# The skip term written by ScalarE, and the graph hops by Horner's rule

## The reference

```python
x = x + gnn(layernorm(x), adj, ...)
x = x + ffn(layernorm(x), ...)

def gnn(X, A, Wv, bv, aw, ab, Wk, bk):          # 3 hops
    Xw = X @ Wv + bv
    sj, si = Xw @ aw[:d, 0], Xw @ aw[d:, 0]
    e = leaky_relu(sj[:, None, :] + si[:, :, None] + ab[0], 0.2)
    alpha = A * exp(e)
    transition = alpha / (alpha.sum(-1, keepdims=True) + 1e-12)
    H, Xk = 0, X
    for k in range(3):
        H = H + Xk @ Wk[k] + bk[k]
        Xk = transition @ Xk
    return relu(H)

def ffn(...):                                   # fc1, Mamba, fc2
    u, z = split(W_in (W_fc1 x + b_fc1));  u = silu(causal_conv4(u) + conv_b)
    dt, B, C = split(W_xproj u);  delta = softplus(W_dt dt + b_dt)
    h_t = exp(delta_t A) h_{t-1} + delta_t u_t B_t        # 1024 channels x 16 states
    y_t = C_t h_t + D u_t;  y = y * silu(z)
    return W_fc2 W_out y + b_fc2
```

## Time and profile before

| | us |
|---|---|
| three runs | 4127.19, 4118.02, 4119.69 |
| median | 4119.69 |
| the profiled execution: its time | 4124.45 |
| its span, from the first to the last instruction | 4122.3 |
| mean granted PE clock | 0.95 of full speed |

### The profile page before, as it was taken

The page is one execution under the profiler, slowest core; times in us unless marked ns, Lnnn a source line. Parts: engine busy times, 40 slices in busy tenths (PEclk is TensorE's granted clock), DMA queues, the critical chain, the costliest instruction groups (busy, mean ns, idle before and its releaser), DMA issues. The chain is left out here.

```text
span 4122.3 us, 44370 instructions
## 1 busy us (share of the span) xinstructions
PE 3597.6 (87%) x11386; PEld 2046.1 (50%) x11386; DVE 3607.9 (88%) x3165; ACT 2868.8 (70%) x6098; POOL 3455.2 (84%) x1860
## 2 busy tenths in 40 slices
PE   6888888988888988888988888988888988888887
PEld 3644554545554545554544554554554554554443
DVE  0499988999989999889998989999999899989898
ACT  1577667777667777667777667777767777767775
POOL 0298888898888998888998888898888898888899
PEclk8899999999999999999999999999999999999999
DMA  2111101111101111101111101111101111101110
GB/s 100 49 51 53 53 9 47 50 53 53 53 8 48 50 53 53 53 8 48 50 53 53 53 8 48 50 53 53 53 9 47 50 53 53 53 8 44 47 47 8
DMA packets 50702, 183.68 MB, mean 45 GB/s; under 512 B 7339, under 2 KB 33203, under 8 KB 42067
## 3 DMA queue, kind: packets, MB, share of 16 engines
q1 hardware_dynamic: 48880, 174.17, 11.0%
q10 hardware_dynamic: 1636, 7.83, 0.5%
HBM read 164.15 MB, written 17.83 MB: 44 GB/s over the span
## 5 line engine op out<-in xcount | busy, mean ns | idle before, releaser
L411 POOL TENSOR_TENSOR st<-st,bc 128x1024 f32<-128x1024 f32 x1024 | 2399.4, 2358 | 474.2 <-DVE st L870 473.0
L870 DVE TENSOR_TENSOR_SCAN st<-dec,st 128x1024 f32<-128x1024 f32 x1024 | 2311.9, 2277 | 78.0 <-ACT dec L464 63.6
L464 ACT ACTIVATE dec<-delta,decay 128x254 f32<-128x254 f32 x4096 | 1695.1, 465 | 713.4 <-DVE st L870 712.4
L685 PE MATMUL y_ps<-st,ident 128*128 128x512 f32 x4096 | 1975.9, 611 | 184.2 <-POOL st L411 182.8
L685 PEld LDWEIGHTS y_ps<-st,ident 128*128 128x128 f32 x4096 | 756.5, 194 | 999.8 <-issue 599.7
L858 DVE TENSOR_TENSOR st<-du,bc 128x1024 f32<-128x1024 f32 x736 | 885.5, 1203 | 34.3 <-ACT du L450 34.3
L402 POOL TENSOR_TENSOR st<-du_sb,bc 128x1024 f32<-128x1024 f32 x288 | 679.3, 2359 | 0.1
L896 DVE SCALAR_TENSOR_TENSOR u<-d_ps,chan,u 128x250 f32<-128x250 f32 (+2 forms) x768 | 309.4, 473 | 160.9 <-ACT u L504 159.2
L705 PE MATMUL g<-wo,zs 128*128 128x256 f32 x1024 | 300.2, 446 | 0.8 <-DVE zs L877 0.8
L705 PEld LDWEIGHTS g<-wo,zs 128*128 128x128 f32 x1024 | 230.8, 229 | 128.8 <-issue 92.1
L681 PE MATMUL y_ps<-u,diag 128*128 128x256 f32 x512 | 168.5, 459 | 127.7 <-DVE zs L877 127.6
(11 more groups left out here) (106 smaller groups left out, 2775.1 us busy)
## 6 DMA issues: line engine op xcount, KB each, us to landing
bc<-bc_dram SPq DMA_DIRECT2D x64, 2048.0 KB, 9.8
xg<-x_dram SPq DMA_DIRECT2D x32, 256.0 KB, 11.5
x_dram<-xg SPq DMA_DIRECT2D x32, 256.0 KB, 2.0
last_x<-x_dram SPq DMA_DIRECT2D x32, 256.0 KB, 2.6
out_dram<-last_x SPq DMA_DIRECT2D x32, 256.0 KB, 2.1
bc<-w_inT_dram ACTq DMA_DIRECT2D x1, 4096.0 KB
adjt<-adjT_dram SPq DMA_DIRECT2D x32, 128.0 KB, 11.2
bc<-w_out_dram ACTq DMA_DIRECT2D x1, 2048.0 KB
```

The costliest lines, as they stand in the source:

```text
L411: nc.gpsimd.tensor_tensor(st[:, sl, :, :, :], st[:, sl, :, :, :], bc[:, p, 1, SU * q:SU * q + SU, None, :].to_broadcast([P, SU, 2, T]), AL ...
L464: a = nc.scalar.activation(dec[:, v % 2, s, j, :].rearrange("p (b t) -> p b t", b=PAIR)[:, :, 1:], delta[:, p, 2 * i + j, :].rearrange("p ...
L685: mm = nc.tensor.matmul(y_all, ident[:, :], st[:, sl, s, :, :].rearrange("p j t -> p (j t)"), start=False, stop=(q == Q - 1 and s == SU - ...
L870: nc.vector.tensor_tensor_scan(h, dec[:, v % 2, :, :, :].rearrange("p s j t -> p (s j t)"), h, 0.0, ALU.mult, ALU.add).then_inc(S["scanned ...
```

## The change

The skip term: at step 2 of each sum, behind the decays of that step, ACT writes `D u` for two channel blocks straight into `y_ps` with two Copy activations (`skip_term`), and PE's first identity matmul of the sum waits for that instead of for the gate. One matmul at the start (`prime`) has written all of the bank once, so that the identity matmuls add. `diag` and its construction go.

The graph stage: with A the attention divided by its row sums, H = b + X W0 + A (X W1 + A (X W2)). PE makes `X W2` (phase 9), ACT copies it (11), the logits move to phase 12, their two Exp to 14, maximum and product on DVE behind the scan of phase 15. The row sums are taken with a 128x128 matrix of ones (17), so that each partition holds them; DVE adds the small constant, takes the reciprocal and multiplies the attention, three operations on 128x256 (19, before the scan). `X W1 + A (X W2)` follows (21, 22), its copy (24), then `b + X W0 + A (...)` (25, 26), and DVE makes `x1` in one operation (28, before the scan). The row sums, the scaled copies and the transposed hops of before go.

```diff
@@ -49,6 +49,8 @@
 FOLD_OUT = (1, 3, 5, 7)
+PRIME_STEP = 25
+SKIP_STEP = 2
 EDGE_STEP = 8
...
@@ -449,6 +447,18 @@
+            def skip_term(act, k, p, i):
+                if i == 0:
+                    wait(act, "silu_u", k + 1)
+                    if isinstance(k, int) and k == 0:
+                        act.wait_ge(S["y_primed"], 1)
+                wait(act, "y_gated", JP * k + i)
+                for j in range(2):
+                    a = nc.scalar.activation(y_ps[:, j, :], u[:, p, 2 * i + j, :], ACT.Copy,
+                                             scale=chan[:, TAPS + 2, 2 * i + j:2 * i + j + 1])
+                a.then_inc(S["skipped"], 1)
             def decays(act, k, p, v):
                 i, q = v // Q, v % Q
@@ -474,6 +484,8 @@
                         decays(act, k, p, v + 1)
+                    if scan and v % Q == SKIP_STEP:
+                        skip_term(act, k, p, v // Q)
                     if dense:
...
                     if scan and v == SILU_Z:
@@ -546,10 +558,7 @@
                     wait(act, "rstd_made", 2 * g + 1 + second)
-                    if second:
-                        wait(act, "h_mm", g + 1)
-                    else:
-                        wait(act, "transposed", 2 * g)
+                    wait(act, "transposed", 2 * g + second)
                     for b in range(PAIR):
...
                                                  scale=rstd[:, b:b + 1])
@@ -559,31 +568,19 @@
                 if v == 11:
+                    wait(act, "x2k_mm", g + 1)
+                    nc.scalar.activation(x2k[:, :, :].rearrange("p b d -> p (b d)"), g0[:, :], ACT.Copy)\
+                        .then_inc(S["x2k_made"], 1)
+                if v == 14:
                     wait(act, "e_mm", g + 1)
-                    e_ps = g0[:, 0:PAIR * L].rearrange("p (b i) -> p b i", b=PAIR)
-                    nc.scalar.activation(att[:, :, :], e_ps, ACT.Exp, bias=c0[:, 0:1])
-                    nc.scalar.activation(g0[:, PAIR * L:2 * PAIR * L], g0[:, 0:PAIR * L], ACT.Exp, bias=c0[:, 1:2], scale=0.2)\
+                    nc.scalar.activation(att[:, :, :].rearrange("p b i -> p (b i)"), g0[:, 0:T], ACT.Exp, bias=c0[:, 0:1])
+                    nc.scalar.activation(g0[:, T:2 * T], g0[:, 0:T], ACT.Exp, bias=c0[:, 1:2], scale=0.2)\
                         .then_inc(S["e_exp"], 1)
-                if v == 19:
-                    wait(act, "rinv_made", g + 1)
-                    wait(act, "u1_mm", g + 1)
-                    for b in range(PAIR):
-                        a = nc.scalar.activation(x1k[:, b, :], g0[:, b * DIM:(b + 1) * DIM], ACT.Copy,
-                                                 scale=rinv[:, b:b + 1])
-                    a.then_inc(S["x1k_made"], 1)
-                if v == 22:
-                    wait(act, "u1T_mm", g + 1)
-                    nc.scalar.activation(u1T[:, :, :].rearrange("p c t -> p (c t)"), g0[:, :], ACT.Copy)\
-                        .then_inc(S["u1T_made"], 1)
                 if v == 24:
-                    wait(act, "u2T_mm", g + 1)
-                    nc.scalar.activation(u2T.rearrange("p c t -> p (c t)"), g0[:, :], ACT.Copy)\
-                        .then_inc(S["u2T_made"], 1)
-                if v == 26:
-                    wait(act, "h0_mm", g + 1)
+                    wait(act, "x1k_mm", g + 1)
                     nc.scalar.activation(x1k[:, :, :].rearrange("p b d -> p (b d)"), g0[:, :], ACT.Copy)\
-                        .then_inc(S["h0_made"], 1)
+                        .then_inc(S["x1k_made"], 1)
                 if v == 37:
                     wait(act, "transposed", 2 * g + 2)
@@ -648,6 +645,11 @@
+            def prime(pe):
+                wait(pe, "wo_folded", JP)
+                nc.tensor.matmul(y_all, ident[:, :], wxz[:, 0, 0:512], start=True, stop=True).then_inc(S["y_primed"], 1)
             def body(pe, k, p, scan, dense, ends, begins):
...
                 for v in range(U):
@@ -659,6 +661,8 @@
                         fold_wo(pe, v)
+                        if v == PRIME_STEP:
+                            prime(pe)
                     if scan:
...
                             project_out(pe, k - 1, r, OUT_STEPS.get(v, ()), ends)
@@ -673,13 +677,7 @@
                 if q == 0:
-                    wait(pe, "y_gated", JP * k + i)
-                    if isinstance(k, int) and k == 0 and i == 0:
-                        pe.wait_ge(S["diag_made"], J)
-                        pe.wait_ge(S["wo_folded"], JP)
-                    for j in range(2):
-                        nc.tensor.matmul(y_ps[:, j, :], diag[:, 2 * i + j, :], u[:, p, 2 * i + j, :],
-                                         start=(j == 0), stop=False, skip_group_check=True)
+                    wait(pe, "skipped", JP * k + i + 1)
                 wait(pe, "c_times", U * k + v + 1)
...
                     mm = nc.tensor.matmul(y_all, ident[:, :], st[:, sl, s, :, :].rearrange("p j t -> p (j t)"),
@@ -774,6 +772,12 @@
                     for b in range(PAIR):
+                        mm = hop(b, 2, True, True)
+                    mm.then_inc(S["x2k_mm"], 1)
+                if v == 12:
+                    wait(pe, "x2k_made", g + 1)
+                    for b in range(PAIR):
                         for c in range(KC):
...
                             nc.tensor.matmul(g0[:, b * L:(b + 1) * L], wi_rep[:, c, :], cols,
@@ -781,55 +785,39 @@
                     mm.then_inc(S["e_mm"], 1)
-                if v == 15:
+                if v == 17:
                     wait(pe, "alpha_made", g + 1)
-                    for b in range(PAIR):
-                        mm = nc.tensor.matmul(g0[:, b:b + 1], att[:, b, :], one_col[:, 0:1], start=True, stop=True)
-                    mm.then_inc(S["rowsum_mm"], 1)
-                if v == 17:
-                    wait(pe, "rinv_made", g + 1)
-                    for b in range(PAIR):
-                        mm = nc.tensor.matmul(g0[:, b * DIM:(b + 1) * DIM], att[:, b, :], xn[:, b, :],
-                                              start=True, stop=True)
-                    mm.then_inc(S["u1_mm"], 1)
-                if v == 20:
+                    nc.tensor.matmul(g0[:, 0:T], ones[:, :], att[:, :, :].rearrange("p b i -> p (b i)"),
+                                     start=True, stop=True).then_inc(S["rowsum_mm"], 1)
+                if v in (21, 22):
+                    b = v - 21
+                    wait(pe, "att_made", g + 1)
+                    hop(b, 1, True, False)
+                    mm = nc.tensor.matmul(g0[:, b * DIM:(b + 1) * DIM], att[:, b, :], x2k[:, b, :],
+                                          start=False, stop=True, skip_group_check=True)
+                    if b == 1:
+                        mm.then_inc(S["x1k_mm"], 1)
+                if v in (25, 26):
+                    b = v - 25
                     wait(pe, "x1k_made", g + 1)
-                    for c in range(KC):
-                        for b in range(PAIR):
-                            mm = nc.tensor.matmul(g0[:, c * T + b * L:c * T + (b + 1) * L],
-                                                  xn[:, b, c * P:(c + 1) * P], att[:, b, :], start=True, stop=True)
-                    mm.then_inc(S["u1T_mm"], 1)
-                if v == 22:
-                    wait(pe, "u1T_made", g + 1)
-                    for c in range(KC):
-                        for b in range(PAIR):
-                            mm = nc.tensor.matmul(g0[:, c * T + b * L:c * T + (b + 1) * L],
-                                                  x1k[:, b, c * P:(c + 1) * P], att[:, b, :], start=True, stop=True)
-                    mm.then_inc(S["u2T_mm"], 1)
-                if v == 24:
-                    wait(pe, "u2T_made", g + 1)
-                    nc.tensor.matmul(g0[:, :], ones3, bk_row, start=True, stop=False, skip_group_check=True)
-                    for b in range(PAIR):
-                        for c in range(KC):
-                            mm = nc.tensor.matmul(g0[:, b * DIM:(b + 1) * DIM], xT[:, c, b * L:(b + 1) * L],
-                                                  wks[:, 0, c, :], start=False, stop=(c == KC - 1),
-                                                  skip_group_check=True)
-                    mm.then_inc(S["h0_mm"], 1)
-                if v in (27, 28):
-                    b = v - 27
-                    wait(pe, "h0_made", g + 1)
-                    for n in range(2):
-                        for c in range(KC):
-                            mm = nc.tensor.matmul(g0[:, b * DIM:(b + 1) * DIM],
-                                                  (u1T, u2T)[n][:, c, b * L:(b + 1) * L], wks[:, 1 + n, c, :],
-                                                  start=(n == 0 and c == 0), stop=(n == 1 and c == KC - 1))
+                    if b == 0:
+                        nc.tensor.matmul(g0[:, :], ones3, bk_row, start=True, stop=False, skip_group_check=True)
+                    hop(b, 0, False, False)
```

(54 more changed lines are left out.)

## The result

The changed kernel takes 4197.12 us (median of 4 runs, 4195.41 to 4198.13) against 4120.6 for the kernel before in the same comparison: ratio 1.0183, 95% interval 1.0165 to 1.02. It is slower by 76 us, where the prediction had 46 us, inside its range.

The account below looks back on a forecast made before the run. No engine's total bounds the kernel; waits on DVE's clock set the pace. Per pair 6.85 - 2.25 + 0.5 - 3.5 = +1.6 us, over 29 pairs +46 us: median 4166 us, range 4070 to 4235, forecast chance 0.53.

Parts of the forecast that it names:

- a, the exponentials behind Ln: Units 24 to 26: exponentials moved behind Ln keep DVE waiting; scan of 27 only 0.25 us late.
- b, PE's gap: Units 25 to 29: PE idles 5.9 us for ACT's copy, loses 2.7 to lower clock; DVE waits 3.7 for row sum.
- b, the reciprocal: DVE at unit 29: reciprocal on 128x256 takes 2.1 us, the three operations together 2.9 us.
- Rival 2: Reciprocal costs like other operations, three operations 1.24 us: no change, 4118 us; chance 0.12.
- c, the waits of units 30 to 1 are swallowed: DVE's lateness absorbs the waits 0.72 and 1.53 us: -2.25 us a pair, 4.6 late at the first taps.
- d: Unit 2: copies replace the diagonal matmuls at equal time, but PE's longer idle time prolongs its lower clock: +0.5 us.
- e, the gain: Units 3 to 16: `x1` made earlier, PE's 5.36 us stall at the output projection goes: -3.5 us a pair.
- the gates at units 10 and 18 I cost at nothing: Skip copies at these gates elsewhere cost nothing; at 18 they run where PE's diagonal ran, within 0.1 us.
- Rival 1: Row sum in time at unit 29, wait 1.0 us: -1.1 us a pair, 4088 us, up to 4050; chance 0.20.
- W + R - 5.0: Change of a pair in us: W is the wait at unit 29, R the three DVE operations; no loss below 5.0.
- Rival 3: ACT becomes late: copies push the next decays by 0.85 us at three other places, +2.5 a pair, 4239 us; chance 0.15.

Follow-up runs that it names:

- the early row sum: The changed kernel with exponentials, maximum and product, row sum and the three DVE operations moved to earlier phases (13, 14, 15, 17): 4147 us, ratio 1.0078.
- the gap filled: The changed kernel with six idle 128x512 matmuls in PE's 5.8 us gap before the sum of unit 24: 4139 us, ratio 1.0054.
- the fastest version: New graph stage reordered, skip term on PE: 4034 us, ratio 0.9801 to the kernel before; with one POOL addition moved as well, 4029 us, ratio 0.9799.

## Why the prediction was right, and where it was off

- **a, the exponentials behind Ln.** Right: a wait of 2.18 us in the shown pair (2.0 by the working), +1.89 to the gate of 26.
- **b, PE's gap.** Right in place, cause and size: 5.80 us for 5.9 (unit 23 ends at 2133.0 by its row, not at 2132.84, which makes 5.75), the copy pair 0.86 for 0.85, wait for the row sum 107.7/32 = 3.4 for 3.7. That it costs time is shown by two runs, 58 us each. Not seen was the second way (Z, z bias, decays), which the early row sum shows.
- **b, the reciprocal.** 1.77 us for 2.1. Rival 2 (0.42) is out. The page "VectorE: DVE Perf Modes" of the Trainium skill (section "Walkthrough: the 8-slice pipeline in each mode") led to an estimate of 2.3; the measurement decides, 1766 ns.
- **c, the waits of units 30 to 1 are swallowed.** Wrong in every second pair. At the loop's edge ACT sits idle with nothing to wait for, 3.94 us in the shown pair against 1.82 before, and DVE still waits 1.81 for `du` and 0.36 for the first decays. Averaged over both kinds of pairs 1.25 us of waits are left between the gates of 26 and 2 (0.85 for `du`, 0.40 for decays). That is the +3.28 instead of +2.55, and it hides more: the wait for the row sum (3.39) and the three operations (2.61) came out 0.6 cheaper than my 3.7 and 2.9, so the term of the swallowed waits is 1.3 us a pair off. ACT's idle time at the loop's edge is 51 to 53 us in all, in 13 places, in each of the seven kernels that have both the new graph stage and ACT's copies, and 25 to 27 in each of those with one or neither. Why it takes both is open.
- **d.** Equal instead of +0.5, but not because the copy is free there: with the graph stage alone this stretch is 0.9 us shorter than with the copies. What the graph stage gains there and what the copies cost cancel, and I had neither; the wait for the second taps is 3.21 to 3.34 us in the shown pairs.
- **e, the gain.** Right: -4.37 for -4.0, and one line takes it back. The decays of unit 12 wait 1.07 for the 0.95 that I had. The step that failed is "the gates at units 10 and 18 I cost at nothing": DVE comes to gate 18 three us earlier, POOL does not, and 0.57 and 1.47 us are waited there, in alternate pairs. By stretches this is the largest error: gate 10 to gate 18 at +1.75 for +0.5, 1.25 us a pair or 36 us of the kernel, where the whole miss is 31 us (4197 - 4166); the other places nearly cancel, +0.73 from the gate of 26 to the taps of unit 1 against 1.0 in a, d and e. That the total is within 31 us is in part luck.
- **Rivals.** Rival 1 wanted the row sum in time, by PE at the upper level or by an earlier copy. Each of these was tried alone (4139 and 4139), and the row sum put ahead of all that (4147): none beats the kernel before. With the gap filled the condition of rival 1 is met almost exactly, a wait of 1.10 us for its 1.0, but the time is 4139 and not 4088. So the constant in W + R - 5.0 was too large: the change itself has 3.39 + 2.61 - 2.55 = 3.45; the difference is the 1.3 of c and 1.25 more from gate 10 to gate 18, less what the stretches of a, d and e came out better. A pair of these remedies together was not tried. It took the reordering of the whole graph stage as well (4111 with ACT's copies, no difference from before). Rival 3 (ACT late at the other three places) did not happen: waits for decays fell from 63.6 to 55.5 us. Against the graph stage alone, where they are 12.4, the copies do add to them, but mostly at unit 12, which the forecast had (1.07 a pair).

## What to carry to other kernels

A producer moved to another engine is priced by its place in that engine's queue, not by its duration: 0.86 us of copies behind two groups of decays kept PE idle for 5.8 us, and 53 to 58 us of the loss were the lower clock behind that idle time. Where a change has two halves, run each alone first; here one was worth -59 us and the other +141. A sum of places can come out near the total while single places are wrong: check it place by place. A stall taken away gives back part of its gain at the next place where another in-order engine (POOL here) has no idle time.

## What the runs showed of the hardware

- The granted clock: behind 5.80 us of idle time the sum took 3.78 us, and 1.98 behind 1.28 us with useless matmuls in between; six such matmuls a pair made the whole kernel 58 us faster (53 by the ratios). In the graph stage alone PE is idle for 3.12 to 3.30 us behind the gate of 26, and the diagonal matmuls that follow take 1.1 to 1.2 us in 26 of 28 pairs, the upper level; in the shown pair of before they take 2.08 behind 2.68 us. So the length of the idle time alone doesn't tell at which level the next row runs. Mean granted clock 0.927 in the change, 0.949 with the gap filled, 0.98 in the fastest version.
- The reciprocal on 128x256 takes 1766 ns where the addition beside it takes 432; on 128x2 it took 166. (1766 - 166)/254 is 6.3 ns a column, an estimate that takes the fixed part as equal for the two.
- ACT writes PSUM from SBUF with a scale for each partition in 467 ns for 128x256 (mean of 256), and the copies that read PSUM of that size take 471 and 472.
